# Moving the low part of the differences between VectorE's two row maxima in an attention kernel

## The reference

```python
scores = jnp.einsum('bhtd,bhsd->bhts', q, k) / SCALING
probs = jax.nn.softmax(scores, axis=-1)
probs = probs.reshape(b, H, 2, t, t)
diff = probs[:, :, 0] - lam * probs[:, :, 1]
attn = jnp.einsum('bhts,bhsd->bhtd', diff, v)
```

## Time and profile before

| | us |
|---|---|
| median of 3 runs (3773.36, 3785.35, 3784.87) | 3784.87 |
| the profiled execution's own time | 3773.84 |
| its span, first to last instruction | 3772.2 |
| what lies around the span | 1.6 |
| PE busy (of the span) | 3272.1 (87%) |
| DVE busy | 2437.2 (65%) |
| ACT busy | 2021.2 (54%) |
| POOL busy | 1684.5 (45%) |

### The profile page before, as it was taken

The page is one execution under the profiler, slowest core; times in us unless marked ns, Lnnn a source line. Parts: engine busy times, 40 slices in busy tenths (PEclk is TensorE's granted clock), DMA queues, the critical chain, the costliest instruction groups (busy, mean ns, idle before and its releaser), DMA issues. The chain is left out here.

```text
span 3772.2 us, 58211 instructions
## 1 busy us (share of the span) xinstructions
PE 3272.1 (87%) x17666; PEld 2628.6 (70%) x17666; DVE 2437.2 (65%) x3685; ACT 2021.2 (54%) x3514; POOL 1684.5 (45%) x2191
## 2 busy tenths in 40 slices
PE   8999977899899989898999962799999999999980
PEld 6888865676666666676776752678788888788870
DVE  6777756888888888888888841444444444444434
ACT  2222216777777777777777730444444444444434
POOL 0000001056566666566666675255444555455542
PEclk9999988999999999999999985899999999999995
DMA  7666674455555455455455411556555556555548
GB/s 250 224 219 225 228 231 108 123 146 135 123 145 134 131 138 136 124 142 138 132 132 146 132 58 56 159 151 180 157 144 157 162 153 181 157 145 163 162 112 360
DMA packets 329154, 594.18 MB, mean 158 GB/s; under 512 B 38032, under 2 KB 136912, under 8 KB 324320
## 3 DMA queue, kind: packets, MB, share of 16 engines
q1 hardware_dynamic: 290784, 524.18, 45.6%
q0 software_dynamic: 35840, 50.60, 7.6%
q10 hardware_dynamic: 2304, 16.78, 1.1%
HBM read 406.13 MB, written 185.53 MB: 157 GB/s over the span
## 5 line engine op out<-in xcount | busy, mean ns | idle before, releaser
L739 DVE TENSOR_REDUCE att_neg_max<-att_ps_s 128x1 f32<-128x1024 f32 x512 | 606.0, 1216 | 80.9 <-PE att_ps_s L532 76.3
L644 ACT ACTIVATE att_prob<-att_ps_s,att_neg_max 128x1024 f32<-128x1024 f32 x512 | 571.1, 1116 | 121.9 <-DVE att_neg_max L739 105.1
L1023 POOL TENSOR_TENSOR exp_w_lo<-exp_w_raw,exp_w_hi 128x2816 fp32r<-128x2816 f32 x63 | 401.6, 6375 | 268.6 <-ACT exp_w_hi L1014 268.6
L532 PE MATMUL att_ps_s<-att_k,att_q 64*128 64x512 f32 x3072 | 436.2, 416 | 63.0 <-ACT att_prob L644 26.2
L827 POOL DMA_INDIRECT slots<-att_entry,att_slot x384 | 397.9, 1036 | 154.7 <-issue 98.6
L532 PEld LDWEIGHTS att_ps_s<-att_k,att_q 64*128 64x128 f32 x3072 | 281.5, 189 | 176.2 <-issue 133.2
L492 PE MATMUL att_ps_t<-att_ident,att_diff 128*128 128x128 f32 x2048 | 275.0, 278 | 80.8 <-ACT att_diff_lo L591 80.5
L686 DVE SCALAR_TENSOR_TENSOR att_diff<-att_prob,att_weight 128x1024 f32<-128x1024 f32 x256 | 332.3, 1298 | 7.1
L492 PEld LDWEIGHTS att_ps_t<-att_ident,att_diff 128*128 128x128 f32 x2048 | 225.9, 141 | 124.3 <-issue 116.7
L591 ACT CAST att_diff_lo<-att_ps_t 128x512 fp32r<-128x512 f32 x256 | 150.2, 587 | 246.5 <-PE att_ps_t L479 246.4
L76 PE MATMUL exp_ps_ab<-exp_x_t_hi,exp_sw_hi 128*128 128x512 f32 x704 | 281.5, 400 | 0.0
(11 more groups left out here) (214 smaller groups left out, 8829.5 us busy)
## 6 DMA issues: line engine op xcount, KB each, us to landing
exp_w_raw<-in_w_t SPq DMA_DIRECT2D x64, 1408.0 KB, 6.2
att_k<-k_parts SPq DMA_DIRECT2D x260, 256.0 KB
att_v<-v_parts SPq DMA_DIRECT2D x64, 1024.0 KB, 5.6
att_q<-q_parts SPq DMA_DIRECT2D x260, 128.0 KB
v_parts<-proj_v_out SPq DMA_DIRECT2D x64, 512.0 KB, 3.3
exp_w_raw<-in_w_t SPq DMA_DIRECT2D x64, 512.0 KB, 3.9
proj_x_raw<-in_x_t SPq DMA_DIRECT2D x17, 1024.0 KB, 7.1
q_parts<-proj_out_hi SPq DMA_DIRECT2D x64, 256.0 KB, 3.3
```

What stands on the lines that cost most here:

```text
L532: last = nc.tensor.matmul(ps_s[s][:, cols], q_buf[q % 2][rows, q_part, q_cols], k_buf[q % 2][rows, k_part, cols], start=m == 0, stop=m == 2)
L644: nc.scalar.activation(prob[s][i][:], ps_s[s][:], ACT.Exp, bias=neg_max[:, s, i : i + 1], accum_out=total).then_inc(exp_done[s], 1)
L739: nc.vector.tensor_reduce(neg_max[:, s, i : i + 1], ps_s[s][:], AX.X, ALU.max, negate=True).then_inc(max_done[s], 1)
L1023: engine.tensor_tensor(w13[1][:], w13_raw[:], w13[0][:].bitcast(F32), ALU.subtract).then_inc(w13_lo_done, 1)
```

## The change

In DVE's list the subtraction that makes the lower half of the low part no longer stands at the head of a turn but between the two row maxima; with remainder 2 the routing's L718 and L720 come behind it. Nothing else changes: the instructions, their waits and the other engines' lists are the same. In the turns behind the last scores, which have no row maxima, the subtraction comes behind the reciprocal.

```diff
             for jl in turns(mode):
                 piece = jl % QT
                 n, k, pair = tile(b, jl, OUT)
-                if live(mode, jl, LOW):
-                    _, q = quad(b, jl, LOW)
-                    t = (jl - LOW) % QT
-                    own = (slice(None), slice(0, HALF_TILES), slice(t * P, t * P + P))
-                    dve.wait_ge(hi_done, STEPS * b + jl - LOW + 1)
-                    nc.vector.tensor_tensor(diff_lo[q % 2][own], ps_t[:, 0:HALF_TILES, :], diff_hi[q % 2][own].bitcast(F32), ALU.subtract).then_inc(lo_done, 1)
                 if piece == 1 and live(mode, jl, OUT):
...
                 if live(mode, jl, 0):
                     row_max(dve, b, jl, 0)
+                if live(mode, jl, LOW):
+                    _, q = quad(b, jl, LOW)
+                    t = (jl - LOW) % QT
+                    own = (slice(None), slice(0, HALF_TILES), slice(t * P, t * P + P))
+                    dve.wait_ge(hi_done, STEPS * b + jl - LOW + 1)
+                    nc.vector.tensor_tensor(diff_lo[q % 2][own], ps_t[:, 0:HALF_TILES, :], diff_hi[q % 2][own].bitcast(F32), ALU.subtract).then_inc(lo_done, 1)
                 if piece == 2 and live(mode, jl, ROUTE):
                     dve_route(dve, b, jl, 1)
                 if live(mode, jl, 0):
                     row_max(dve, b, jl, 1)
```

## The result

The changed kernel takes 3924.18 us (median of 4, 3919.9 to 3925.87). Against the runs of the kernel before, taken with it, the ratio is 1.0367, with a 95% interval of 1.0345 to 1.0389: slower by 3.7%. The forecast was 3921. The profiled execution went from 3773.84 to 3925.8 us, by 152.0, where the sum said 136.6; that the median agrees to 3 us is in part luck, since the profiled execution of the kernel before lay 11 us under its median and that of the changed one 1.6 us above.

What follows compares the result with a forecast made beforehand. PE was taken to set the pace, held up by chains starting at the scores. 57 cycles give 131.7 us, less 8 and 3.6, plus 16.5: 136.6 us on 3784.87, forecast 3921 us, range 3888 to 3962.

Steps and rivals of the forecast that it cites:

- signs that were to show it wrong: A cycle under 26 or over 28 us, L492's wait still naming ACT, or a falling clock.
- (a): PE's transposes wait for the later subtraction: +0.78 us in remainder 3, +0.93 in remainder 2, 0.30 absorbed in remainder 0.
- (b): The second maximum and its exponential come 0.60 us later on DVE and ACT; remainder 0 pays +0.60 us.
- Remainder 1: Turns forecast to cost nothing: the output product covers the transposes; cover before the next scores shrinks from 0.81 to 0.21 us.
- A cycle: Four turns of the attention stage, forecast to grow by 2.31 us, from 24.91 to 27.2 us.
- rival 3: Faster: with DVE the bound, waits for `hi_done` vanish and the first exponential starts earlier; up to 50 us gained, chance 0.02.
- L541's wait: PE's wait for `score_exp`, forecast to grow from 0.77 to about 1.3 us.
- POOL's norms: In 14 cycles they hold up an exponential and cover part of the delay: 8 us off, from 5.5 to 10.
- Early turns: Turns 3 to 27, before the output part is complete: 16.5 us more in all.
- lower bound of 115: The forecast sum in us with the low ends of its terms, where a cycle grows by 2.15 us.
- rival 1: PE's idle gaps of up to 1.7 us make the clock fall: 3948 or 4000 us, chance 0.08.
- the loop's returns: Six standstills of DVE where the order of ready instructions costs no 0.60 us: 3.6 us off the sum.

Runs made afterwards that it cites:

- mid_rem3: Kernel before, with the subtraction between the maxima only in turns of remainder 3, at the head in the others; 3820.12 us, ratio 1.0106.
- extra_between: Kernel before, its subtraction still at the head, plus an extra unused subtraction of the same size between the maxima in batches 1 to 7; 3861.77 us, ratio 1.0209.
- mid_rem0: Kernel before, with the subtraction between the maxima only in turns of remainder 0, at the head in the others; 3810.01 us, ratio 1.0087.
- mid_rem2: Kernel before, with the subtraction between the maxima only in turns of remainder 2, at the head in the others; 3820.07 us, ratio 1.0103.
- mid_rem1: Kernel before, with the subtraction between the maxima only in turns of remainder 1, at the head in the others; 3794.39 us, ratio 1.0037.

## Why the prediction was right, and what it missed

The mechanism was right and stands on experiments, not on the time alone. Two of the signs that were to show it wrong did appear, in six of the 57 cycles: the clock fell there, and a cycle with such a turn takes 28.8 us.

- **Remainder 3, (a).** +0.78 forecast, +0.77 in the changed kernel and in mid_rem3. extra_between shows that the second maximum has no part in it.
- **Remainder 2, (a).** +0.93 forecast, +0.91 measured: transposes 3.77 instead of 2.86 us into the turn.
- **Remainder 0, (b).** +0.60 forecast, +0.60 in the changed kernel, +0.59 in mid_rem0. The earlier start of the next instruction decides as the trace before said; a subtraction's full 0.69 us would have been too much.
- **Remainder 1.** Nothing forecast, -0.01. The thin cover of 0.21 us held.
- **A cycle.** 27.2 us forecast, 27.20 usual. The idea that a first maximum could come earlier (rival 3) fell: DVE's waits for `hi_done` did disappear, but those for the scores grew by 128 us.
- **L541's wait.** I had said 1.3 us; it is 0.93. The transposes and value products ahead of it slip by 0.3 us, as (a) has it for remainder 0, and take that much out of the wait. I had the number and didn't subtract it; the turn's length isn't touched.
- **POOL's norms.** 8 us off, in the range 5.5 to 10. In the 14 cycles remainder 3 grew by 0.34 instead of 0.77 us and remainder 0 by 0.35 instead of 0.59, in all 9.3 us.
- **Early turns.** 16.5 forecast, 17.5 measured, and the agreement is partly luck. Turns 0 to 6 grew by 4.4 us and not 2.4, turn 6 alone by 2.9 with a granted clock of 0.56 where it had 0.82; turns 7 to 27 grew by 13.1 and not 14.1, mostly because turn 8, for which I had 0.60, didn't grow.
- **Slips in the working.** The subtraction is out 1.81 us behind the start of the maxima, not 2.0; the times given there are right. The lower bound of 115 doesn't come out of its terms: 57 x 2.15 - 10 - 3.6 + 16.5 = 125.5. An early cycle would grow from 23.5 to 26.3, not 26.1.

Two terms were missing or wrong. First, the clock, rival 1, which had 0.08. It did not replace the forecast but came on top: six turns of 1.6 us, 9.6 us. I had judged by the busy share of a stretch (85% against 79% at full clock) and not by the single longest wait in it. Turns 7 to 24 of the changed kernel, with 70% and waits of 1.5 us, have no slow turn, nor has mid_rem2 with 1.53 us, though its cycle is otherwise that of the kernel before. Second, the loop's returns. I had expected them cheaper by 3.6 us; the twelve turns around the six returns grew by 10.0 us, where without my correction it would have been 6 x (0.77 + 0.59) = 8.2. At one of them (1004.04 to 1013.99) the granted clock is 0.52 and a turn takes 9.95 us. The returns differ by -0.4 to +3.7 us each. PE's standstill ahead of the scores there ("issue" in the waits), a fourth wait that the prediction left out, is nearly the same in sum, 13.5 us where it was 13.3, so it doesn't make the difference; how much of it the clock makes stays open. Once a batch DVE also stands still for 0.24 us ahead of a maximum in remainder 2 with nothing visible that it waits for; these seven turns are 0.34 us longer, 2.4 us in all.

The sum as it came, from turn 28 on, with the means of the turns that none of these effects touches: 57 x (0.59 + 0.91) + 56 x 0.775 = 128.9 for remainders 0, 2 and 3, -0.9 for remainder 1, -9.3 for POOL, +1.8 at the returns against that, +9.6 clock, +2.4 pauses, and 17.5 before: 150.0.

## What to carry to other kernels

Before an instruction moves in an in-order queue, look for the wait of the instruction that it is moved behind: here the new place made an old result wait for new scores, and through one buffer that exists only once, that held PE. Price each turn of the loop by its own last arrival; the same move cost 0, 0.6, 0.8 and 0.9 us in the four turns, according to which arrival it met. And when a change makes the longest wait of PE longer, count on the clock too: look at the single wait and not only at the mean busy share, and when a sure gain doesn't show, look at the turns one by one.

## What the hardware showed that I had not expected

The granted clock fell in some turns although PE was busy for about 86% of a cycle; before, with waits of at most 0.8 us in the usual turns, it stayed at 1.00 there, and in the changed kernel it did so with 70% and 1.5 us in every turn. In the changed kernel the wait was 1.7 us in 50 turns of remainder 2, of which six were slow, and 2.0 us in the seven with DVE's pause, of which none was; with a cycle shorter by 0.67 us it was 26 and 25 in two runs, nearly every other one, so the fall depends on more than the wait's length. What picks the turns stays open. Work without use in a wait took time off: six matmuls 16 us off the stage, ten matmuls 128 us off the kernel's time. And a DVE instruction on one column, started while POOL's L794 ran, took 0.7 us instead of 0.21 and ended with it, 13 times in mid_rem1.
